# A cross-attention query stage on one Trainium2 core: the turn of a tile moved among the mixing groups of the next, and the queries' eviction moved from DVE to ACT

## The reference

```python
tgt = tgt + self_attention(layernorm(tgt, n1))     # ends with  out @ sa_out_w.T + sa_out_b
x = layernorm(tgt, n2_g, n2_b)                     # over the 512 channels of a token
q = x @ wq.T + bq                                  # wq, bq: the first third of ca_in_w, ca_in_b
scores = q @ k.T / sqrt(32)                        # 16 heads, keys from the context
tgt = tgt + softmax(scores) @ v @ ca_out_w.T + ca_out_b
```

## Time and profile before

| | us |
|---|---|
| median of three executions | 3193.87 (3188.46 to 3200.21) |
| the profiled execution, its time | 3189.28 |
| the profiled execution, its span | 3187.6 |
| the c_ stage, first mixing to the last projection's end | 1163.9 to 1439.7 |
| PE busy in that stretch | 229.6 of 275.8, mean granted clock 0.91 |
| PE busy in the whole span | 2980.7 (94%) |

### The profile page before, as it was taken

One profiled execution on the slowest core, in us unless ns is written; L12 is line 12 of the kernel. 1 busy time (PEld: TensorE's weight loads), 2 busy tenths in 40 slices (PEclk: granted clock), 3 DMA queues, 4 the chain that ended last, 5 costly groups with the idle time before them and its releaser, 6 DMA issues.

```text
span 3187.6 us, 39475 instructions
## 1 busy us (share of the span) xinstructions
PE 2980.7 (94%) x15242; PEld 1966.3 (62%) x15242; DVE 1758.3 (55%) x2864; ACT 1243.5 (39%) x2335; POOL 1907.5 (60%) x991
## 2 busy tenths in 40 slices
PE   7999999999999959789999999999879999999999
PEld 6888886444444427664444444444348888888887
DVE  4455656777777535666777777777742222222221
ACT  2212222555555533325666666666532111111111
POOL 3324333888888775437888888888768343333432
PEclk8999999999999979999999999999989999999999
DMA  6555774445455135734234242332122101011000
GB/s 208 176 165 186 227 220 127 107 108 111 108 117 116 41 119 184 212 133 105 63 72 89 54 104 57 79 82 58 54 67 89 40 27 40 14 40 33 34 14 14
DMA packets 199538, 310.17 MB, mean 97 GB/s; under 512 B 15011, under 2 KB 93363, under 8 KB 199347
## 3 DMA queue, kind: packets, MB, share of 16 engines
q1 hardware_dynamic: 199350, 307.64, 35.3%
HBM read 189.04 MB, written 117.44 MB: 96 GB/s over the span
## 4 chain that ended last, share of the span: by engine, by line
PE 53%; DVE 5%; DMA 2%; POOL 1%; issue 1%; ACT 1%; SPq 1%; DVEq 0%; POOLq 0%; ACTq 0%
PE m_ring L89 13%; PE m_o_ps L89 10%; PE e_st L1217 8%; PE e_pv L1229 7%; PE e_nat L1200 7%; PE c_ring L89 5%; PE e_st L1241 2%; DVE e_neg_max L1110 2%; DMA e_qs<-e_max_lo 1%; DMA c_x<-in_x 1%; DVE m_xt_lo L1577 1%; DMA c_w_raw<-in_ca_in_w 0%; DVE m_xt_hi L1575 0%; DVE m_ow_lo L1595 0%; DVE m_xn L1570 0%
## 5 line engine op out<-in xcount | busy, mean ns | idle before, releaser
L1054 POOL TENSOR_TENSOR e_probs<-e_probs 128x2048 f32<-128x2048 f32 x160 | 732.7, 4585 | 146.5 <-ACT e_probs L1029 141.7
L1029 ACT ACTIVATE e_probs<-e_st 128x512 f32<-128x512 f32 x1024 | 558.1, 598 | 361.5 <-PE e_st L1217 344.0
L1110 DVE TENSOR_REDUCE e_neg_max<-e_nat 128x1 f32<-128x1024 f32 x512 | 603.0, 1217 | 141.6 <-PE e_nat L1200 136.7
L1029 ACT ACTIVATE b_probs<-b_st 128x512 f32<-128x512 f32 (+3 forms) x768 | 340.4, 491 | 278.6 <-PE b_st L1217 269.5
L1107 DVE CUSTOM_DVE_ANT_0 b_nat<-b_nat,mask_qk 128x128 f32<-128x128 f32 (+7 forms) x512 | 374.4, 784 | 80.8 <-PE b_nat L1200 79.6
L1217 PE MATMUL e_st<-e_qs,e_ks 98*128 98x512 f32 x1024 | 396.3, 431 | 22.6 <-DVE e_turned_sums L1128 12.3
L1545 POOL TENSOR_TENSOR m_hid_lo<-m_hid,m_hid_hi 128x512 fp32r<-128x512 f32 x128 | 168.3, 1315 | 386.5 <-DVE m_hid_hi L1583 386.5
L1054 POOL TENSOR_TENSOR b_probs<-b_probs 128x1536 f32<-128x1536 f32 (+3 forms) x128 | 374.7, 2927 | 38.0 <-PE b_pv L1229 35.1
L1583 DVE CAST m_hid_hi<-m_hid 128x512 fp32r<-128x512 f32 x128 | 60.4, 472 | 575.4 <-ACT m_hid L1459 575.4
L1200 PE MATMUL e_nat<-e_ks,e_qs 96*128 96x512 f32 x1024 | 327.5, 401 | 26.2 <-DVE e_neg_max L1110 26.2
L1217 PEld LDWEIGHTS e_st<-e_qs,e_ks 98*128 98x128 f32 x1024 | 176.2, 189 | 275.9 <-ACT e_probs L1029 188.7
(11 more groups left out here) (182 smaller groups left out, 5164.0 us busy)
## 6 DMA issues: line engine op xcount, KB each, us to landing
b_qs<-sq_hi SPq DMA_DIRECT2D x32, 512.0 KB, 6.7
b_ks<-sk_hi SPq DMA_DIRECT2D x32, 512.0 KB, 11.1
e_qs<-cq_hi SPq DMA_DIRECT2D x32, 512.0 KB, 6.8
e_ks<-ck_hi SPq DMA_DIRECT2D x32, 512.0 KB, 13.4
ck_hi<-p_part_hi SPq DMA_DIRECT2D x32, 256.0 KB, 3.3
ck_lo<-p_part_lo SPq DMA_DIRECT2D x32, 256.0 KB, 3.7
cv<-p_tok_out SPq DMA_DIRECT2D x32, 256.0 KB, 3.0
p_x<-in_x SPq DMA_DIRECT2D x8, 1024.0 KB, 7.4
```

The lines of the kernel that those rows point to most:

```text
L1029: act.activation(probs[:, home(n, k), j, first:TOK], st_ps[:, bank_at("scores", blk), first:TOK], ACT.Exp).then_inc(exped, 1)
L1054: pool.tensor_tensor(into, into, probs[:, home(n, k), :, first:TOK], ALU.add).then_inc(added, 1)
L1110: dve.tensor_reduce(neg_max[:, u:u + 1], found, AX.XY, ALU.max, negate=True).then_inc(maxed, 1)
```

## The change

In `order`, the turns of tile i are spread: two before mix(i+1, 0), one before mix(i+1, 1), one before mix(i+1, 2). For tile 0 the mixings 0 and 1 of tile 1 come first, then norm(0), and the turns follow between and behind mixings 2 and 3. The bias of tile i+1, piece u, moves on POOL from the turns into mix(i+1, u), ahead of the subtraction of c_o's piece u. The projections' eviction leaves DVE: ACT reads the bank twice, with the scale and a bias that was multiplied by the scale once before, and writes c_full and the rounded c_part_hi. `emptied` is gone; `hi_ready`, set by the second of the two, frees the bank.

```diff
     def order(self, mix, aggregate, norm, turn, chan, beside):
         for u in range(SUB):
             mix(0, u)
         aggregate(0)
-        norm(0)
-        for c in range(KC):
-            turn(0, c)
         for i in range(TILES):
-            if i + 1 < TILES:
-                for u in range(SUB):
+            turned = 0
+            for u in range(SUB):
+                if i == 0 and u == 2:
+                    norm(0)
+                while turned < (u - 1 if i == 0 else u + 2) and turned < KC:
+                    turn(i, turned)
+                    turned += 1
+                if i + 1 < TILES:
                     mix(i + 1, u)
                     beside(i, u)
+            while turned < KC:
+                turn(i, turned)
+                turned += 1
+            if i + 1 < TILES:
                 aggregate(i + 1)
             for k in range(KC):
                 chan(i, k)
                 beside(i, SUB + k)
                 if k == 1 and i + 1 < TILES:
                     norm(i + 1)
-            if i + 1 < TILES:
-                for c in range(KC):
-                    turn(i + 1, c)
...
# ACT
         def chan(i, k):
-            act.wait_ge(self.emptied, i * KC + k + 1)
-            act.copy(self.part_hi[:, k, :], self.full[:, k, :]).then_inc(self.hi_ready, 1)
+            seq, (m, scale, _, _) = self.chan_seq(i, k), self.chans[k]
+            act.wait_ge(self.filled, seq + 1)
+            if i >= 1:
+                act.wait_ge(self.part_stored[k], 32 * i)
+            for out in (self.full, self.part_hi):
+                last = act.activation(out[:, k, :], self.ring[:, seq % self.RING, :], ACT.Identity,
+                                      bias=self.scaled_bias[:, m:m + 1], scale=scale)
+            last.then_inc(self.hi_ready, 1)
...
# POOL
         def mix(i, u):
+            if i >= 1:
+                bias(i, u)
             if i + 1 < TILES:
                 split_o(i + 1, u)
-        def turn(i, c):
-            if i + 1 < TILES:
-                bias(i + 1, c)
...
# DVE
-        def chan(i, k):
-            seq = self.chan_seq(i, k)
-            dve.wait_ge(self.filled, seq + 1)
-            if i >= 1:
-                dve.wait_ge(self.part_stored[k], 32 * i)
-            self.chans[k][0](dve, self.full[:, k, :], self.ring[:, seq % self.RING, :], i % HALVES).then_inc(self.emptied, 1)
-
+        dve.tensor_scalar(self.scaled_bias[:], self.q_bias[:], self.chans[0][1], None, ALU.mult).then_inc(self.bias_scaled, 1)
...
# PE
-                pe.wait_ge(self.emptied, was - sum(m < was for m in mixes) + 1)
+                pe.wait_ge(self.hi_ready, was - sum(m < was for m in mixes) + 1)
...
-                pe.wait_ge(c.emptied, TILES * KC)
+                pe.wait_ge(c.hi_ready, TILES * KC)
                 e_lead("start")
```

More of the change, by code:

```diff
@@ L512, with __init__ @@
     RING, PARTS = 4, 4
-    def __init__(self, place, sem, ident, o_src, ow, o_bias, x_src, x_dst, norm, w, chans):
+    def __init__(self, place, sem, ident, o_src, ow, o_bias, x_src, x_dst, norm, w, chans, q_bias):
         self.ident, self.o_src, self.x_src, self.x_dst, self.chans = ident, o_src, x_src, x_dst, chans
@@ L533, in __init__ @@
         at = SMALL_AT
+        self.q_bias, self.scaled_bias = q_bias, place("c_scaled_bias", at + 1664, [P, KC])
         self.gb, self.stats = place("c_gb", at, [P, 2, KC]), place("c_stats", at + 32, [P, SUB, 6])
@@ L539, in __init__ @@
         self.w_loaded, self.w_hi_done, self.w_lo_done = [sem(f"w_loaded{k}") for k in range(8)], sem("w_hi_done"), sem("w_lo_done")
+        self.bias_scaled = sem("bias_scaled")
         self.ow_lo_done = sem("ow_lo_done")
@@ L545, in __init__ @@
         self.turned, self.turned_out, self.x_lo_done = sem("turned"), sem("turned_out"), sem("x_lo_done")
-        self.filled, self.emptied, self.hi_ready, self.lo_ready = sem("filled"), sem("emptied"), sem("hi_ready"), sem("lo_ready")
+        self.filled, self.hi_ready, self.lo_ready = sem("filled"), sem("hi_ready"), sem("lo_ready")
         self.part_stored = [sem(f"part_stored{k}") for k in range(self.PARTS)]
@@ L598, in store @@
             n = i * KC + k
-            _, hi, lo = self.chans[k]
+            _, _, hi, lo = self.chans[k]
             sp.wait_ge(self.hi_ready, n + 1)
@@ L670, in scalar @@
         act.wait_ge(self.small_loaded, 16 * 3)
+        act.wait_ge(self.bias_scaled, 1)
         split(range(KC, 2 * KC))
@@ L711, in gpsimd @@
                                ALU.subtract).then_inc(self.w_lo_done, 1)
-        self.order(mix, aggregate, lambda i: None, turn, chan, beside)
+        self.order(mix, aggregate, lambda i: None, lambda i, c: None, chan, beside)
     def vector(self, dve, beside):
@@ L756, in vector @@
                               ALU.subtract).then_inc(self.ow_lo_done, 1)
-        self.order(mix, aggregate, norm, turn, chan, beside)
+        self.order(mix, aggregate, norm, turn, lambda i, k: None, beside)
     def tensor(self, pe, beside):
@@ L1831, in first_stages, with last_stages @@
         sem.clear()
-def last_stages(nc, place, a, ident, cross_q, tokens, att_home, chan_home, by_group, qk, vals, att, x1, y):
+def last_stages(nc, place, a, ident, q_bias, cross_scale, tokens, att_home, chan_home, by_group, qk, vals, att, x1, y):
     with ExitStack() as ctx:
@@ L1840, in last_stages @@
                    tokens(a["x"]), tokens(x1), (a["n2_g"], a["n2_b"]), a["ca_in_w"][:, 0:D],
-                   [(cross_q(m), chan_home(qk["cq_hi"], m), chan_home(qk["cq_lo"], m)) for m in range(KC)])
+                   [(m, cross_scale, chan_home(qk["cq_hi"], m), chan_home(qk["cq_lo"], m)) for m in range(KC)], q_bias)
         C_ITEMS = c.chan_seq(TILES - 1, KC - 1) + 1
@@ L2018, in self_k @@
             return dve.tensor_tensor(out, psum, keep[:, s * TOK:(s + 1) * TOK], ALU.mult)
-        def cross_q(m):
-            return lambda dve, out, psum, s: dve.tensor_scalar(out, psum, q_bias[:, m:m + 1], cross_scale,
-                                                               ALU.add, ALU.mult)
         def cross_k(m):
@@ L2028, in layer @@
                      chan_home, by_group, qk, vals, att)
-        last_stages(nc, place, a, ident, cross_q, tokens, att_home, chan_home, by_group, qk, vals, att, x1, y)
+        last_stages(nc, place, a, ident, q_bias, cross_scale, tokens, att_home, chan_home, by_group, qk, vals, att, x1, y)
 def kernel(**inputs):
```

## The result

The kernel after takes 3199.35 us in the median of 20 executions (3193.57 to 3206.31), the one before 3194.15 (3184.92 to 3200.21, also 20): a ratio of 1.0018, with a 95% interval of 1.001 to 1.0025. That is 0.2% slower, told from zero but within the 0.5% bound, so "no change" by the text above; the forecast was 3194.1 and its range 3184 to 3206. The profiled execution has a span of 3197.7 us against 3187.6. Times and ratios in this document are those of fast executions: one of e10's four, 3703.4 us at a mean granted clock of 0.744, is left out, and e7's and e8's single ones (0.973 and 0.972, as in the fast ones) are taken as they are.

A forecast was written before the change was run, and what follows sets the result against it. PE, busy for 94% of the span, was taken as the bound. Gains at the start and losses in later blocks summed to +1.1 us, set against a mean of 3193.0: 3194.1 us, range 3184 to 3206.

The forecast's parts named there:

- The start: Stage's start: tile 1's mixings 0 and 1 fill PE's wait for the norm, which ends later; -3.0 us.
- Blocks 1 and 2: Tiles 1 and 2, between last projections: PE waits for x_lo behind c_o's rounding; -0.5 and 0.0 us.
- The price of the shared port: In blocks 1 and 2, each DVE subtraction making c_x_lo takes 1.0 us more beside busy POOL.
- half of a slow stretch: In blocks 1 and 2, PE's lower clock after idle gaps was charged at 0.8 us.
- Blocks 3 to 5: Tiles 3 to 5: quarter 3 falls behind the c_x-bound second e_nat pair, and e_nat 3 may stall; +1.1 us each.
- block 6: Tile 6: the turn's quarter 3 stands behind the c_x wait, but no c_o is loaded; +0.5 us.
- Block 7: Last tile's block: the turns start on ACT 0.2 us later and PE still waits for them; +0.2 us.
- Hand-over: From the last projection to the attention's first scores: ACT's paired eviction frees the bank later; +0.6 us.
- (a): Rival, faster: c_x does not hold blocks 3 to 6; -36 us, 3157 at the full; chance 0.05.
- (b): Rival, partly hidden: no port waits or second slow stretch in the start, blocks 1 and 2; -9 us, 3184; chance 0.07.
- (c): Rival, slower: POOL, ACT and DVE in lockstep, second slow stretch in every block; +22 us, 3215; chance 0.07.
- (d): PE's wait for the turn only moves behind c_x; the forecast's own mechanism, given no separate chance.

The follow-up runs named there:

- e10: Kernel after with DVE evicting the projections as before, and the loads of c_x and c_o both issued early: 3161.36 us, 0.9886 of before.
- e7: Kernel after with only POOL's order changed, four biases ahead of the four differences: 3195.99 us in one execution, before at 3195.16.
- e8: Kernel after with only ACT's order changed, c_o's four roundings behind the turn's last eviction: 3214.61 us in one execution, before at 3195.16.
- e3: Kernel after with ACT's c_o roundings behind the turn's last eviction and POOL's biases ahead of its differences, from tile 2 on: 3191.17 us, 0.9991 of before.
- e5: Kernel before with the load of c_x issued at the block's start, not behind its stores: 3181.11 us, 0.9949 of before.
- e2: Kernel after with DVE evicting the projections as before, so the new order alone: 3205.22 us, 1.0033 of before.
- e1: Kernel before with only the projections' eviction moved to ACT, all orders old: 3191.46 us, 0.999 of before.
- e6: Kernel after with the loads of c_x and c_o both issued early: 3162.82 us, 0.99 of before.
- e11: Kernel after with c_x loaded early and c_o issued behind the block's last store: 3179.84 us, 0.994 of before.
- e9: Kernel before, old order, with the loads of c_x and c_o both issued early: 3177.77 us, 0.9935 of before.
- e4: Kernel after with only c_o's load issued earlier, ahead of the block's stores: 3196.91 us, 1.0013 of before.

## Why the prediction was right, and where its terms were off

The changes below are those of the profiled executions, after minus before, from the table.

**The start: -3.0 forecast, -3.1 measured.** The norm ended at 1196.89 in a trace whose stage begins 2.5 us later than that of before, so at 1194.4 on the time scale of before; forecast 1194.5. It stood behind the join of tile 1's mixing 1, and this behind POOL's bias and difference, as said. Of the rest two terms were off and cancelled: the last x_lo cost PE 0.8 us of waiting, not 2, and slow time cost 3.0 us, not 1.6 (the granted clock was 0.50 from 1197 to 1201 and 0.80 from 1201 to 1205). That the start came out to 0.1 us is luck in this part.

**Blocks 1 and 2: -0.5 and 0.0 forecast, +2.5 and +3.2 measured.** This is the step that was mis-sized. Its mechanism (rounding ahead of quarter 2, POOL's alternation, x_lo as the last release) is what the chain shows and what e3, e7 and e8 confirm by taking it apart, but three terms were too small. In block 1 the last x_lo ended at 19.2 us, not 18.0: 1.0 of that is c_o, which landed 12.6 us in and not 11.6 (its load took 9.00 us). The other 0.2 is a net of small ones. The forecast put one of the two x_lo on the path, and the chain has both: the join of mixing 1 began at 16.3 us, where c_o's delay alone gives 15.8, because the x_lo of quarter 2, long by its own wait, still held DVE. Then PE took 11.5 us from there to the end, not 9.7 (8.9 and half of a slow stretch): the low clock came whole, in both blocks, and reached past projection 0. 1.2 and 1.8 make the 3.0 between 27.7 and 30.7. The price of the shared port itself was right: each x_lo was 1.0 to 1.1 us longer. The norm does not reach into the next block, as I had it: it ended at 1248.1 and the block at 1250.1; one of the two idles was put in the wrong place, and both occur ahead of x_lo instead. Both blocks lie outside the bounds that the forecast gave them (+0.3 and +0.8).

**Blocks 3 to 5: +1.1 each forecast, +2.0, +1.7 and +1.1 measured; block 6: +0.5 and +0.6.** Right in kind. In block 5 the second pair of e_nat starts 12.6 us in and the idle time ahead of it was 4.81 us (forecast 4.7). I had quarter 3 at 0.55; at the low clock it is 0.85, and the pair 1.22 in place of 0.73. e5 shows the cause by removing it: with c_x early these blocks lose 2.1 to 8.3 us even in the old order. The other half of this step fell: no block of 4 and 5 has a second stall, for e_nat 3, and the low clock pays instead. The chain of block 4 in the kernel after, which in that of before reads 0.73 and 4.34 us from 13.1 us in, without a quarter of the turn:

```profile
1336.17 1.22 PE e_nat L1207 x2
1337.39 0.85 PE c_tr L796 x4
1338.25 4.79 PE c_ring L89 x12
```

That is 6.86 us in place of 5.07, again from 13.1 us in: 1.8, the block's 1.7. In block 5 the same three are 6.22, so +1.1. Block 3, where PE also waits 4.55 us for the attention's first loads, was not taken apart; its +2.0 is above the forecast's 1.7, and block 4 is at it.

**Block 7: +0.2 forecast, -0.3 measured.** An eviction of the ring is shorter than one of the turn's bank, so that a pair takes 1.26 us, not 1.44, and the turns do not start later. The other 0.3 goes with DVE's queue, which has no eviction any more: PE's wait for the last maxima fell from 1.04 to 0.85 us, and the block takes 20.70 us in e2 with the new order and DVE's eviction, 20.40 in e1 with the old order and ACT's. ACT's rows of the kernel after:

```profile
1219.41 0.69 ACT L677 ACTIVATE c_full<-c_ring,c_scaled_bias 128x512 f32<-128x512 f32 x1 [1.46 <-PE c_ring L89]
1219.99 0.68 ACT L677 ACTIVATE c_part_hi<-c_ring,c_scaled_bias 128x512 fp32r<-128x512 f32 x1
```

**Hand-over: +0.6 forecast, +0.5 measured.**

**The sum: +1.1 forecast, +8.3 in the profiled execution and +5.2 in the medians.** It lies in the forecast's own bounds (-7 to +10), near their upper end, and the excess is nearly all of blocks 1 and 2, which gave 5.7 us where their bounds end at 1.1. That the whole still lies inside is in part luck: other terms left their upper bounds unused (the start -3.1 against +1, block 7 -0.3 against +0.5). What holds is the mechanism, and that the gains and the losses nearly cancel. No rival took place. (a) failed by its own reason, since the c_x chain does bind blocks 3 to 6; the runs put its price well: it gave blocks 4 to 6 at 27.8 and blocks 1 and 2 at 24, and e6, with both loads early, has 27.7 in blocks 4 and 5, 28.8 in block 6, and 23.6. It asked for c_x 4.7 us earlier and overlooked that c_o must come earlier too, which e11 shows. (b) failed on the clock and on the ports. (c), the lockstep of POOL, ACT and DVE, was seen for a step or two, with one slow stretch in the blocks and not two. (d), that PE's wait only moves, is what happened in blocks 3 to 6; in blocks 1 and 2 the wait became a longer one with another source, two waits of 1.97 and 0.68 us turned into 2.30 and 1.96.

**What stays open** is when the clock falls. In e1, block 2, PE had the old order's turn waits (1.82 and 0.68 us) and kept 1.00; in block 1 of the same run it had the same two waits, and the clock was 0.50 from 1228 to 1230. In before, block 2, it had 1.97 and 0.55, and the block's mean was 0.94. In e1, block 5, even a wait of 3.19 us ahead of e_nat left the clock at 1.00 from 1361.5 to 1374. The same gaps are followed by a slow stretch in one place and by none in another, and a stretch is worth 1.3 to 1.8 us a block. Nor was it tried whether after's blocks 1 and 2 would lose their slow stretch with c_o landing as before.

## What to carry to other kernels

Before work is interleaved, list for each engine what the moved instruction will stand behind, and follow that instruction back to its DMA: on queues that keep their order a cast for three tiles ahead can put a load into today's path, and it can do so through two engines at once. A reorder that seems to gain nothing may be a gain that a late load hides; trying both orders with the loads early (e10 and e6 beside e9) tells the two apart, and both loads must be early together, as e4 shows. Price a slow stretch of the clock whole in the upper bound of each block where the change leaves PE waiting, and not at half: it came whole in both blocks here, and e1 shows that it can as well stay away.

## What the runs showed of the hardware

The port showed from both sides: an x_lo of 0.69 us took 1.75 and the POOL subtraction that it met 1.74 in place of 1.3, while the joins between them, which read one tensor from PSUM and one from SBUF, stayed at 0.68 us with POOL busy. The Trainium skill ("SBUF — State Buffer", section "Who interferes with whom") says the same, that a DVE instruction with two SBUF inputs contends with one of GpSimd that reads SBUF, and that one with a single SBUF input, outside the modes that use both of DVE's ports, does not: the trace agrees, with these numbers. And in e6, where nothing of PE's waits for them, the x_lo take as long (1.70 and 1.73 in block 1), and the block still lasts 23.6 us.

The tiny scaled bias, which I had at nothing, was long for its size. DVE's row in the kernel after:

```profile
1157.69 3.49 DVE L759 TENSOR_SCALAR c_scaled_bias<-q_bias 128x4 f32<-128x4 f32 x1 [4.34 <-PEq L75]
```

It is 4 elements a partition, where c_var of the same shape took 0.17 us at 1242.96 with POOL idle, and it lasts 3.49 us beside a memset of 3.52 on POOL that began at 1157.65 (the chain has it as `e_ks`); it is 3.49 us beside the same memset in all nine traces that have it. The same section says that a tensor_scalar may take both of the shared ports, and that the engine that comes second then waits for the other's whole instruction; the two ends, 1161.18 and 1161.17, agree with it. Nothing waited for this one, so it cost nothing here.
